# Moving the bulk transfers of an attention layer to GpSimd's queue, and the low halves of q and k to the front of VectorE's step

## The reference

```
q, k, v = x1 @ Wq.T, x1 @ Wk.T, x1 @ Wv.T           # split into 16 heads
a = q @ k.T * 512**-0.5 + (adj + adj)               # per head, 512 x 512
o = softmax(a) @ v
out = layernorm(x1 + o @ Wo.T)
```

## Time and profile before

| | |
|---|---|
| median of 3 runs | 2613.17 us (2611.36 to 2617.87) |
| the profiled execution, its own time | 2616.51 us |
| its span, first to last instruction | 2614.9 us |
| TensorE matmul busy | 2273.9 us, 87% |
| VectorE, ScalarE busy | 1611.0 us, 62%; 1613.9 us, 62% |
| GpSimd busy | 432.9 us, 17% |
| DMA queue of Sync | 256.96 MB, 53.4% of 16 DMA engines' span |
| DMA queue of GpSimd | 37.76 MB, 4.6% |
| mean granted TensorE clock | 0.936 of 2.4 GHz |

### The profile page before, as it was taken

One profiled execution on the slowest core, in us unless ns is written; L12 is line 12 of the kernel. 1 busy time (PEld: TensorE's weight loads), 2 busy tenths in 40 slices (PEclk: granted clock), 3 DMA queues, 4 the chain that ended last, 5 costly groups with the idle time before them and its releaser, 6 DMA issues.

```text
span 2614.9 us, 49332 instructions
## 1 busy us (share of the span) xinstructions
PE 2273.9 (87%) x14947; PEld 1793.5 (69%) x14947; DVE 1611.0 (62%) x4043; ACT 1613.9 (62%) x3589; POOL 432.9 (17%) x728
## 2 busy tenths in 40 slices
PE   6888888868989888988898889889998989898987
PEld 5677767756767666766776667767776767676764
DVE  6556666546566656665656566666666666665655
ACT  4334333437667666766676767666666676666765
POOL 4222222111020202020111111111111110112011
PEclk9988888979999999999999999999999999999999
DMA  5332222276757485757485857575766676666662
GB/s 205 136 109 96 96 96 96 81 127 115 125 102 130 97 131 97 130 98 132 96 136 96 137 93 140 99 130 100 136 99 130 100 138 106 124 111 122 110 96 55
DMA packets 147621, 297.75 MB, mean 114 GB/s; under 512 B 13074, under 2 KB 13106, under 8 KB 147250
## 3 DMA queue, kind: packets, MB, share of 16 engines
q1 hardware_dynamic: 135954, 256.96, 53.4%
q0 software_dynamic: 11424, 37.76, 4.6%
HBM read 110.12 MB, written 50.33 MB: 61 GB/s over the span
## 4 chain that ended last, share of the span: by engine, by line
PE 51%; DMA 14%; issue 7%; DVE 4%; SPq 3%; ACT 2%; POOL 0%; DVEq 0%; POOLq 0%; ACTq 0%
PE bank L675 21%; PE bank L721 13%; DMA qp<-stage_q 10%; PE bank L690 8%; PE bank L705 7%; DMA adj_sb<-in_adj_dram 4%; SPq L383 3%; DVE prob L1247 2%; PE bank L713 1%; ACT prob L963 1%; DVE stage_q L1035 1%; PE bank L647 1%; ACT probT L840 1%; PE bank L655 1%; DVE z L1286 0%
## 5 line engine op out<-in xcount | busy, mean ns | idle before, releaser
L1247 DVE CUSTOM_DVE_ANT_0 prob<-bank,adj_sb 128x512 f32<-128x512 f32 x1024 | 657.8, 686 | 319.4 <-PE bank L690 249.9
L840 ACT ACTIVATE probT<-bank 128x512 f32<-128x512 f32 x832 | 461.1, 594 | 484.2 <-PE bank L721 481.3
L963 ACT ACTIVATE prob<-prob,neg_max 128x512 f32<-128x512 f32 x1024 | 731.0, 723 | 11.7 <-DVE neg_max L1256 9.3
L721 PE MATMUL bank<-ident,prob 128*128 128x128 f32 x4096 | 548.1, 277 | 9.2 <-ACT probT L840 9.1
L721 PEld LDWEIGHTS bank<-ident,prob 128*128 128x128 f32 x4096 | 473.2, 142 | 116.5 <-issue 62.3
L690 PE MATMUL bank<-kp,qp 128*128 128x512 f32 x1024 | 371.3, 446 | 205.3 <-DMA qp<-stage_q 121.7
L690 PEld LDWEIGHTS bank<-kp,qp 128*128 128x128 f32 x1024 | 187.5, 202 | 251.6 <-issue 178.8
L1261 DVE COPY probT<-bank 128x512 f32<-128x512 f32 x192 | 132.0, 688 | 295.2 <-PE bank L721 256.6
L705 PE MATMUL bank<-probT,v 128*32 128x256 f32 x4096 | 257.5, 394 | 0.1
L589 PE MATMUL bank<-zT,w_sel 128*128 128x512 f32 x768 | 220.0, 450 | 3.0 <-ACT w_sel L840 3.0
L675 PE MATMUL bank<-xT,wqT 128*128 128x512 f32 x768 | 221.5, 428 | 0.0
(11 more groups left out here) (119 smaller groups left out, 2495.8 us busy)
## 6 DMA issues: line engine op xcount, KB each, us to landing
kp<-stage_k SPq DMA_DIRECT2D x256, 256.0 KB, 7.0
qp<-stage_q SPq DMA_DIRECT2D x256, 256.0 KB, 7.5
adj_raw<-in_adj_dram SPq DMA_DIRECT2D x16, 1024.0 KB, 7.2
x_raw<-in_x_dram SPq DMA_DIRECT2D x16, 1024.0 KB, 9.1
outT_spill<-outT SPq DMA_DIRECT2D x16, 1024.0 KB, 5.2
v<-outT_spill SPq DMA_DIRECT2D x16, 1024.0 KB, 13.2
z<-in_x_dram POOLq DMA_DIRECT2D x64, 256.0 KB, 3.0
adj_sb<-in_adj_dram SPq DMA_DIRECT2D x64, 256.0 KB, 8.4
```

Of the source, the lines that this page charges most:

```text
L721: ins = nc.tensor.transpose(t_bank[j % 2][:, mt * P:(mt + 1) * P], prob[:, s % 2, j, mt * P:(mt + 1) * P], ident[:, :])
L840: return nc.scalar.activation(dst, src, ACT.Copy, scale=scale)
L963: nc.scalar.activation(prob[:, s % 2, j, :], prob[:, s % 2, j, :], ACT.Exp, scale=2.0, bias=neg_max[:, s % 2, j:j + 1], accum_out=row_sum[ ...
L1247: nc.vector.tensor_tensor_reduce(prob[:, s % 2, j, :], s_bank[j][:, :], adj_sb[:, t, :], 1.0, LOWEST, ALU.add, ALU.max, row_max[:, g % 2, ...
```

## The change

Four things, all in layer 1:

1. `load_yT`, `load_adj`, `spill_x1` and `load_x1` move from Sync's stream to GpSimd's, with the same waits. Sync keeps the packs alone. On GpSimd `load_yT` stands in step 1, `spill_x1` in step 10, `load_adj` in steps 12 to 15 and `load_x1` in step 13. The layer norm of the output tile now precedes `softmax_weights` in a step.
2. q of group 2 goes from step 5 to step 4, and output tile 3 from step 4 to step 5. `O_ADDED`, `O_NORMED` and `X_LOADS` follow: tile 3 is added in step 6, normalised and stored in step 7, and its x for the next batch is loaded in step 8. `Y_STEPS` stays.
3. `stage_low` comes first in VectorE's step, ahead of `copy_probT` and `bias_and_max`.
4. The ReLU of layer 0's result on ScalarE goes from steps 1 to 3 to steps 2 to 4.

```diff
 SLOTS = ([("k", 2, 0)]
-         + [("o", 0, -1), ("o", 1, -1), ("o", 2, -1), ("o", 3, -1), ("q", 2, 0), ("k", 3, 0), ("q", 3, 0)]
+         + [("o", 0, -1), ("o", 1, -1), ("o", 2, -1), ("q", 2, 0), ("o", 3, -1), ("k", 3, 0), ("q", 3, 0)]
...
-RELU_STEPS = {1: (0,), 2: (1, 2), 3: (3,)}
+RELU_STEPS = {2: (0,), 3: (1, 2), 4: (3,)}
...
             def batch(b, par, first, last):          # Sync
-                if not last:
-                    load_yT(b + 1, 1 - par)
                 for s in range(STEPS):
                     kind, i, rel = SLOTS[s]
                     if kind in "kq" and is_live(s, first, last):
                         pack(kind, b + rel, i)
-                    if s == 9 and not last:
-                        spill_x1(b + 1)
-                    if s >= 12 and not last:
-                        load_adj(b + 1, s - 12, True)
-                    if s == 13:
-                        load_x1(b, last)
...
             def batch(b, par, first, last):          # GpSimd
                 for s in range(STEPS):
+                    if s == 1 and not last:
+                        load_yT(b + 1, 1 - par)
                     if s in X_LOADS and not last:
                         load_x(b + 1, X_LOADS[s], first)
+                    if s == 10 and not last:
+                        spill_x1(b + 1)
+                    if s >= 12 and not last:
+                        load_adj(b + 1, s - 12, True)
+                    if s == 13:
+                        load_x1(b, last)
+                    if s in O_ADDED and not first:
+                        layer_norm_rstd(1, b - 1, O_ADDED[s], f_mv, f_eps, f_rstd)
                     if s % NT == 3:
                         softmax_weights(b, s // NT)
-                    if s in O_ADDED and not first:
-                        layer_norm_rstd(1, b - 1, O_ADDED[s], f_mv, f_eps, f_rstd)
                     if s in O_NORMED and not first:
                         store_out(b - 1, O_NORMED[s])
                     if s in Y_STEPS and not last:
...
+                    if kind in "kq" and there:       # VectorE, first in the step
+                        stage_low((s - 1) % STEPS, b + rel)
                     if s > 0 and s - 1 not in ACT_COPIES_3:
                         copy_probT(b, s - 1, 3)
                     elif s == 0 and not first:
                         copy_probT(b - 1, STEPS - 1, 3)
                     if ahead:
                         bias_and_max(nb, ns, (0, 1, 2))
-                    if kind in "kq" and there:
-                        stage_low((s - 1) % STEPS, b + rel)
                     if ahead:
                         bias_and_max(nb, ns, (3,))
```

More of the change, by code:

```diff
@@ L360, in _ @@
             spill_outT(B - 1)
[L363 to L371, removed]
             def pack(m, b, g):
@@ L384, in pack @@
                                  f32(src[:, :])).then_inc(packed[m], 16)
[L386 to L397, removed]
-            layer0_over(sp)
[L400 to L404, removed]
+            layer0_over(sp)
             for g in range(2):
@@ L514, in load_x, with load_adj, load_yT, spill_x1 @@
                 pool.dma_start(z[:, t, :], row_tile(x, b, t)).then_inc(x1_x_in[t], 16)
+            def load_adj(b, t, reused):
+                if reused:
+                    wait_apart(pool, s_max, 64 * (b - 1) + J * (12 + t) + J)
+                pool.dma_start(adj_sb[:, t, :], row_tile(adj, b, t)).then_inc(adj1_in[t], 16)
+            def load_yT(b, par):
+                wait_apart(pool, pv_ps, 8 * (b - 1))
+                pool.dma_start(v[:, par, :, :], rows(outT_dram, b)).then_inc(yT_in, 16)
+            def spill_x1(b):
+                wait_apart(pool, x1_done, NT * b + NT)
+                pool.dma_start(rows(x1_dram, b), z[:, :, :]).then_inc(x1_spilled, 16)
+            def load_x1(b, last):
+                if last:
+                    for t in range(NT):
+                        wait_apart(pool, out_stored[t], 16 * b)
+                else:
+                    wait_apart(pool, x1_spilled, 16 * (b + 2))
+                    wait_apart(pool, xT_ps, NT * (b + 2))
+                pool.dma_start(z[:, :, :], rows(x1_dram, b)).then_inc(x1_back, 16)
             layer0_over(pool)
+            load_yT(0, 0)
             for t in range(NT):
@@ L519, in _ @@
             for t in range(NT):
+                load_adj(0, t, False)
+            for t in range(NT):
                 layer_norm_rstd(0, 0, t, y_mv, y_eps, y_rstd)
+            spill_x1(0)
             def batch(b, par, first, last):
                 for s in range(STEPS):
+                    if s == 1 and not last:
+                        load_yT(b + 1, 1 - par)
                     if s in X_LOADS and not last:
                         load_x(b + 1, X_LOADS[s], first)
+                    if s == 10 and not last:
[6 more added lines that the diff above has]
+                        layer_norm_rstd(1, b - 1, O_ADDED[s], f_mv, f_eps, f_rstd)
                     if s % NT == 3:
                         softmax_weights(b, s // NT)
-                    if s in O_ADDED and not first:
-                        layer_norm_rstd(1, b - 1, O_ADDED[s], f_mv, f_eps, f_rstd)
                     if s in O_NORMED and not first:
@@ L1316, in batch @@
                     gb, gg = (b, s // NT - 1) if s > 0 else (b - 1, G - 1)
+                    if s > 0:
+                        (kind, i, rel), there = SLOTS[s - 1], is_live(s - 1, first, last)
+                    else:
+                        (kind, i, _), rel, there = SLOTS[STEPS - 1], 0, not first
+                    if kind in "kq" and there:
+                        stage_low((s - 1) % STEPS, b + rel)
                     if s > 0 and s - 1 not in ACT_COPIES_3:
```

## The result

The changed kernel takes 2682.85 us in the median of 4 runs (2678.7 to 2687.98), against 2614.07 before on the same chip: a ratio of 1.0263, 95% interval 1.0239 to 1.0287. It is 69 us slower. The forecast was 2641, 28 us slower. The direction and the two large prices were right, and the forecast rise came out at less than half of the measured one.

The account below looks back on a forecast made before the run. TensorE's work plus its gaps was taken to bound the kernel. The terms -126 - 45 - 13 + 97 + 6 + 113 gave +32 us, taken as +28 after a clock correction: 2641 us, 8-in-10 range 2548 to 2685.

Parts of the forecast that it names:

- the two large prices: Predicted costs of the low halves first, 97 us, and of the later output tile, 113 us.
- What bounds the kernel: Whole kernel: a step is as long as TensorE's work plus its gaps; TensorE is busy 87% of the span.
- The 2.4 us which I called latency: Pack transfers: some 2.4 us of latency on top of 8.2 us for 1 MB, from a lone 256 KB store.
- The wait before step 8: Scores of step 8: q of group 2 a step earlier removes the pack wait and its clock cost, -126 us.
- The adjacency: Nine batches with a late adjacency tile: off Sync's queue the tiles land before use, -45 us.
- the 0.93: Layer 0's transpose in step 5: its wait for an output tile's addition goes in 14 batches, -13 us.
- Low halves first: Eight steps with q or k: `stage_low` first delays TensorE, 6.5 us in a batch, +97 us in all.
- What the later output tile does: Tile 3, steps 7 to 9: store and load land behind packs, costing 8.1 us in 14 batches, +113 us.
- Rival A: Chance 0.28: faster, since the load of x isn't held by the pack; tile term 18 us, time 2546 us.
- What GpSimd's queue does: Batch end: loads ahead of group 0's q pack lengthen its wait by 0.4 us, +6 us in 15 batches.
- C: Rival, chance 0.12: 1.25 MB hold group 0's q pack longer, its wait grows to 3.2 us; 2687 us.

Follow-up runs that it names:

- experiment 6: Changed kernel with the old slots and the low halves put back, leaving the queue move (and later ReLU): 2708.71 us, ratio 1.0336.
- experiment 5: Kernel before with only the low halves of q and k put first in VectorE's step: 2632.21 us, ratio 1.0063.
- experiment 1: Changed kernel with the low halves put back behind the maxima of heads 0 to 2: 2719.92 us, ratio 1.0404.
- experiment 3: Changed kernel with Sync holding the pack of q of group 3 until x of tile 3 has landed: 2583.67 us, ratio 0.988.
- Experiments 9 and 10: Kernel before with the new slots alone, 2627.54 us; the same with x of tile 3 in its own buffer, loaded a step earlier, 2487.21 us.
- experiment 7: Changed kernel with only the old slots (output tile 3 in step 4, q of group 2 in step 5): 2663.02 us, ratio 1.0176.
- experiment 4: Changed kernel with softmax_weights again ahead of the output tile's layer norm on GpSimd: 2637.93 us, ratio 1.0094.
- experiment 12: Changed kernel with own buffer for x of tile 3, softmax_weights first, low halves behind the maxima, x1 loaded at step 15's end: 2536.53 us.

## Why the prediction was right or wrong

**What bounds the kernel: right.** The gaps were what the edits moved, and each step's length outside a gap stayed to 0.02 us (steps 4, 11 and 12). The 2.4 us which I called latency are those of a whole store of 256 KB, its own bytes included; no later sum uses them, as the 11.1 us of the pack were read from its rows.

**The wait before step 8 (-126, corrected to about -130): right in mechanism, a little small.** With the low halves' own 0.94 us taken out, rows 7 and 8 of the table give 6.75 + 1.43 + 0.94 = 9.1 us a batch, 146 in sixteen. The pack came in time.

**The adjacency (-45) and the 0.93 (-13): sizes right, credit wrong.** 2.86 x 14 = 40 us, and 3 in batch 15. But the wait goes by either edit: experiment 6 shows it for the queues, experiment 5 for the low halves first. Beside these the queues had no gain to set against their price.

**Low halves first (+97): right as a price, wrong as a verdict on the part.** Measured 5.9 us a batch, the 1.4 of steps 1 and 13 as 1.47 and 1.50 (rows 2 and 14). I had not worked out what the earlier issue of each pack is worth once the queues are moved: experiment 1 says more than it costs.

**"What the later output tile does" (+113): right.** 7.6 us a batch, 106 in 14, by the mechanism that was given: store behind one pack, load behind the next. Rival A has fallen, and experiment 3 is the direct evidence. Experiments 9 and 10 show it at 9.7 us a batch, where the low halves come later.

**The step that failed is "What GpSimd's queue does", with its +6 us.** "The issues are cheap and GpSimd is idle" looked at how busy the engine is and not at the order in its stream. Experiments 5 and 7 differ by the move of the queues and its reordering (and the ReLU) alone, at the old slots with the low halves first: 2632.21 and 2663.02, a price of 31 us where the term has 6. In the changed kernel three terms were mis-sized:

- The exchange of layer norm and `softmax_weights` was in the diff and I gave it no price. It is 1.24 us in each batch's step 5, 17 us (experiment 4), and the whole edit cost 45 with the clock's share. With it undone the kernel takes 2637.93, within 3 us of the forecast 2641, but this is partly luck: the errors below, up and down, happen to cancel.
- The wait for group 0 grew as I took it (+0.41, 6 us). But step 0 grew too, by 0.86, 12 us, for which there was no term. It is the clock: in batch 6 step 0 takes 7.02 us in place of 5.44, and the clock is low for half of it. The windows of the changed kernel, batch 6, step 0 (columns as in the earlier trace rows):

```profile
1355.60:1362.60 7.00, 6.93 (x31) 5.74 (x32) 3.38 (x12) 2.65 (x8) 1.74 (x4) 0.76 0.96 131
```

TensorE has gaps of 1.25 and 1.93 us ahead of it, where the kernel before had one of 1.4. But the gaps alone do not decide: in experiment 7 the same step comes after gaps of 1.22 and 1.90 us, the clock stays at 1.00, and it takes 5.44; experiment 4 is like it.

- The start of layer 1, 3.2 us, and the end, 1.7 (36.0 in place of 34.3 from the last scores on), had no term.

A fourth belongs to the output tile: with the normalisation in step 7, VectorE comes late into step 8. Row 9 grew by 1.75 where the low half explains 0.65, so 1.1 us x 14 = 15 us more (experiments 9 and 10 show it too, 10.29 against 9.19).

These make 17 + 12 + 15 + 5 = 49 us. The larger gain before step 8 (-16) and the smaller price of the chain (-7) take 23 of it. From +28 that leads to 54 of the 71.5 us between the two profiled runs. Of the rest, 5.4 is layer 0, which was slower in this run and is none of the change's doing. About 8 lie in batch 15: up to its last scores the terms make it 9.3 us shorter and it got 1.6 shorter, with step 9 alone 3.1 longer. The last 4 or so are small differences of several terms.

Of the rivals, C came nearest in time, by none of its own mechanism: group 0's wait did not grow past 3 us. In experiments 1 and 6, with the low halves behind, the wait does grow, to some 6 us (6.14 in the row of experiment 1). So C was a real risk, which the low halves first averted.

**Still open:** why the clock falls, and stays low longer, after some gaps and not after others of the same length, which moves 1 to 2 us a batch in the changed kernel and in experiments 4 and 12. No run here was made for it.

## What to carry to other kernels

Before a tile is moved by a step, follow what reuses its buffer: here one step later meant a store behind one pack and a load behind the next, and ate 106 us of the 146 gained; 2 KB a partition more would have kept all of it. An engine's idle time says nothing about the order within its stream: an instruction put first delays everything behind it until its own input is there. Moving a transfer to an idle queue doesn't take it out of the way of others; put it where no urgent transfer is due soon, and count what each earlier issue buys before an order that costs TensorE time is undone.

## What the runs showed of the hardware

- Transfers of Sync's and of GpSimd's queue were mostly served in the order of issue while a pack kept the DMA engines busy. A load of 256 KB took 3.0 us or 6.9 depending on whether a pack of the other queue was ahead of it, and while it waited the pack's queue moved 295 packets and its own none; a pack of 1 MB was usable after 11.4 us or 15.8, with 1 MB of the other queue ahead. It is not a rule without exception: in experiment 12 a load of 1 MB, issued 2.1 us behind a pack while both stood behind another megabyte, shared the engines with it, 72% to 31% of their time over 6 us.
- The granted clock can fall after short gaps, but it need not. In the changed kernel's batch 6, step 0 it is down to a mean of 0.76 (partly at 1.2 GHz) after gaps of 1.25 and 1.93 us, some 13 us apart; in experiment 7, after 1.22 and 1.90 us as far apart, it stays at 1.00 in the same step. The kernel before keeps it after a single gap of 1.8.
